# One of four steps issues its first fill ahead of the next block's scores

## The chip, the cores and the metric

The kernel runs on one core of a Trainium2 chip. The metric is the device time of one execution in microseconds (us); the time before is 1831.91 us, the median of 3 runs (1830.47 to 1837.54). Engines are called PE (TensorE), DVE (VectorE), ACT (ScalarE), POOL (GpSimd) and SP (SyncE, which here only issues transfers).

## The reference

```
x = x + 0.5 * ffn(layernorm(x))      # router: softmax, top 8 of 64, bias mix
x = x + attn(layernorm(x))           # gated linear attention with decay, below
x = x + 0.5 * ffn(layernorm(x))

# attn: 32 heads in 8 groups of 4, D = 128, L = 2048 tokens in chunks of 128
q, k, v = rope(x Wq), rope(x Wk), x Wv          # k, v shared by the 4 heads of a group
scores  = q k^T                                 # inside a chunk
y_intra = (scores * decay * dt) v
state   = state * exp(G_last) + (k * decay)^T (v dt)
y_inter = (q * exp(G)) state_of_the_chunk_before
y       = rmsnorm(y_intra + y_inter) * gnorm_w * silu(x Wg)
out     = y Wo
```

## The kernel before

The two ffn parts are a prologue (to about 125 us) and an epilogue (from about 1760 us). Between them stands the attention: for each of the 8 groups g there are 16 chunks n of 128 tokens, so 128 steps. Four chunks are a block b, and s = n mod 4 is the place of a chunk in its block. Every matrix product in bf16 is done as three (`mm3`, lines 298 to 300: high times high, low times high, high times low).

The projections of the next block (keys, four q heads, values, four gate parts) are ten **fills** of 12 matmuls or more each. They are spread over the four steps of the present block by the table `FILLS`: step s = 3 issues fill 8 in slot A and fill 9 in slot B (gate parts). Each fill goes to one of three PSUM banks; it waits until the fill two or three uses before has been read.

On PE a step is, in program order: the scores of chunk n+1 (`scores`), the fill of slot A, the read of the state (`read_state`), four transposes of the gated output of chunk n-1 (`turn_z`, L784), the weighting of the values and the new state (`attend`), the fill of slot B, and the output projection of chunk n-2 (`project_out`).

The names that the steps of the argument touch:
- `scores(g, n + 1)` writes bank `B_S`. At s = 3 chunk n+1 is the first of the next block, so it waits for all of that block's rounded q and k, last for QL of POOL (L1110), the low part of the last q head.
- DVE opens its step with `decayed(g, n + 1)` (L1307, four instructions that read `B_S`), then `add_out` (L1372), and at s = 3 then `keys_lo` (L1298, writes KDL, reads bank `B_T`).
- `B_T` is one bank, and transposed keys and transposed outputs share it. `turn_z(g, n - 1)` on PE waits on `turn_free` (L782); at s = 3 the count that it waits for is that of `keys_lo(b + 1)`.
- All engines run the groups in a hardware loop (`Fori(0, KVH - 1)`) whose body goes from n = 3 to n = 18, that is from step 3 of a group to step 2 of the next. The first instruction of its body is thus an s = 3 step. There are seven rounds: one entry, six turns, and after the exit the last group as straight code.

The order of instructions on each engine is written out by hand; only semaphores tie them together. Nothing is reordered at run time.

Of the kernel before, what the change touches and what calls it, by code (L numbers as in the profile page):

```python
# [29 lines left out]
BLK = 4  # L30
# [40 lines left out]
def filled(n, last):  # L71

    return {} if last and n // BLK == NB - 1 else FILLS[n % BLK]


def use_of(b, item):

    return NFILL * b + item
# [33 lines left out]
def build(nc, x, cos, sin, masks, wall, rwt, rb, eb2, wint, dtb, alog, gn, out):  # L112
    rows_dram = nc.dram_tensor("rows_dram", (NCH, KVH, GW), F32).ap()
    with ExitStack() as ctx:
# [177 lines left out]
        def wl_of(piece):  # L292

            return (wl_pool, POOL_LO.index(piece)) if piece in POOL_LO else (wl_dve, DVE_LO.index(piece))

        def mm3(out_, ah, al, bh, bl, first, last):

            nc.tensor.matmul(out_, ah, bh, start=first, stop=False)  # L298
            nc.tensor.matmul(out_, ah, bl, start=False, stop=False)  # L299
            return nc.tensor.matmul(out_, al, bh, start=False, stop=last)  # L300

        def bank(use):
            return RING[fill_bank(use)]
# [352 lines left out]
        def _(pe):  # L656
# [21 lines left out]
            def wkt(piece, k):  # L678
                return WH[:, piece, k * P:(k + 1) * P], WL[:, piece, k * P:(k + 1) * P]

            def bank_free(g, n, item, use):

                if n is None:
                    if use >= 3:
                        pe.wait_ge(ring_free.sem, ring_free.at(g, use - 3))
                elif n < PEEL:
                    pe.wait_ge(ring_free.sem, ring_free.at(g, use - AFTER_FILL_PEELED[item]))
                elif item in AFTER_FILL:
                    pe.wait_ge(ring_free.sem, ring_free.at(g, use - AFTER_FILL[item]))
                else:  # L690
                    pe.wait_ge(out_free.sem, out_free.at(g, n - 3))

            def fill(g, b, item, n, fresh, gw):

                use = use_of(b, item)
                out_bank = bank(use)
                bank_free(g, n, item, use)
                t0 = b % NB * TB
                if fresh:
                    piece = item if item <= PV_ else PG + KT - 1  # L700
                    pe.wait_ge(wh_ready.sem, wh_ready.at(gw, piece))
                    if item <= PV_:
                        signal, k = wl_of(piece)
                        pe.wait_ge(signal.sem, signal.at(gw, k))
                if item < PV_:
                    for k in range(KT):
                        wh, wl = wkt(item, k)
                        ins = mm3(out_bank[:, :], wh, wl, XTH[:, k, t0:t0 + TB], XTL[:, k, t0:t0 + TB], k == 0, k == KT - 1)
                elif item == PV_:
                    for s in range(BLK):  # L710
                        for k in range(KT):
                            t = t0 + s * P
                            wh, wl = wkt(item, k)
                            ins = mm3(out_bank[:, s * P:(s + 1) * P], XTH[:, k, t:t + P], XTL[:, k, t:t + P], wh, wl,
                                      k == 0, k == KT - 1)
                else:
                    t = t0 + (item - PG) * P
                    for k in range(KT):
                        if fresh and item == PG:
                            signal, i = wl_of(PG + k)  # L720
                            pe.wait_ge(signal.sem, signal.at(gw, i))
                        ins = mm3(out_bank[:, :], XTH[:, k, t:t + P], XTL[:, k, t:t + P], WH[:, PG + k, :], WL[:, PG + k, :],
                                  k == 0, k == KT - 1)
                ins.then_inc(ring_full.sem, 1)

            def turn_keys(g, b):
                if b:
                    pe.wait_ge(turn_free.sem, turn_free.at(g, k_turn(b) - 1))
                pe.wait_ge(qf_ready.sem, qf_ready.at(g, 5 * b))
                for s in range(BLK):  # L730
                    ins = nc.tensor.transpose(B_T[:, s * P:(s + 1) * P], KF[:, s * P:(s + 1) * P], IDF[:, :])
                ins.then_inc(kt_full.sem, 1)

            def scores(g, n):
                b, s = divmod(n, BLK)
                par, t = b % 2, s * P
                if s == 0:
                    pe.wait_ge(qh_ready.sem, qh_ready.at(g, 5 * b + 4))
                    pe.wait_ge(ql_ready.sem, ql_ready.at(g, 3 * b + 2))
                    pe.wait_ge(ql2_ready.sem, ql2_ready.at(g, 2 * b + 1))  # L740
                pe.wait_ge(p_ready.sem, p_ready.at(g, n - 1))
                mm3(B_S[:, :], KH[:, par, t:t + P], KL[:, par, t:t + P], QH[:, par, :, t:t + P], QL[:, par, :, t:t + P],
                        True, True).then_inc(scores_full.sem, 1)

            def read_state(g, n):
                b, s = divmod(n, BLK)
                par, t = b % 2, s * P
                if n % NCH:
                    pe.wait_ge(inter_read.sem, inter_read.at(g, in_event(n - 1)))
                    pe.wait_ge(sth_ready.sem, sth_ready.at(g, cs_event(n - 1)))  # L750
                    pe.wait_ge(stl_ready.sem, stl_ready.at(g, cs_event(n - 1)))
                    for h in range(G):
                        c = slice(h * P, (h + 1) * P)
                        ins = mm3(B_IN[:, c], QH[:, par, h, t:t + P], QL[:, par, h, t:t + P], STH[:, c], STL[:, c], True, True)
                    ins.then_inc(inter_full.sem, 1)

            def attend(g, n):
                b, s = divmod(n, BLK)
                par, t = b % 2, s * P
                pe.wait_ge(z_ready.sem, z_ready.at(g, n - 1))  # L760
                pe.wait_ge(ph_ready.sem, ph_ready.at(g, n))
                pe.wait_ge(pl_ready.sem, pl_ready.at(g, n))
                if s == 0:
                    pe.wait_ge(v_ready.sem, v_ready.at(g, b))
                    pe.wait_ge(ring_free.sem, ring_free.at(g, use_of(b, PV_)))
                for h in range(G):
                    c = slice(h * P, (h + 1) * P)
                    ins = mm3(B_PV[:, c], PH[:, n % 2, c], PL[:, n % 2, c], VH[:, par, t:t + P], VL[:, par, t:t + P], True, True)
                ins.then_inc(intra_full.sem, 1)
                if n % NCH == NCH - 1:  # L770
                    return
                pe.wait_ge(st_ready.sem, st_ready.at(g, cs_event(n - 1)))
                pe.wait_ge(wvh_ready.sem, wvh_ready.at(g, cs_event(n)))
                pe.wait_ge(wvl_ready.sem, wvl_ready.at(g, cs_event(n)))
                if s == 0:
                    pe.wait_ge(kdh_ready.sem, kdh_ready.at(g, b))
                    pe.wait_ge(turn_free.sem, turn_free.at(g, k_turn(b)))
                mm3(B_CS[:, :], KDH[:, par, t:t + P], KDL[:, par, t:t + P], WVH[:, :], WVL[:, :], True, True).then_inc(cs_full.sem, 1)

            def turn_z(g, n, last=False):  # L780
                pe.wait_ge(turn_free.sem, turn_free.at(g, z_turn(n, last) - 1))
                pe.wait_ge(z_ready.sem, z_ready.at(g, n))  # L782
                for h in range(G):
                    ins = nc.tensor.transpose(B_T[:, h * P:(h + 1) * P], YF[:, h * P:(h + 1) * P], IDF[:, :])  # L784
                ins.then_inc(zt_full.sem, 1)
# [34 lines left out]
            def step(g, n, last):  # L820
                b, s = divmod(n, BLK)

                def slot(x):
                    if x in filled(n, last):
                        fill(g, b + 1, filled(n, last)[x], n, b == NB - 1, g + 1)
                if not (last and n == NCH - 1):
                    scores(g, n + 1)
                slot("A")
                read_state(g, n)
                if n:  # L830
                    turn_z(g, n - 1, last)
                attend(g, n)
                if s == 1 and n >= 2:
                    project_out(g, n - 2, last)
                slot("B")
                slot("C")
                if s == 2 and filled(n, last):
                    turn_keys(g, b + 1)
                if s != 1 and n >= 2:
                    project_out(g, n - 2, last)  # L840
# [679 lines left out]
```

## Time and profile before

| what | value |
|---|---|
| median of 3 runs | 1831.91 us |
| profiled execution, device time | 1833.69 us |
| its span, first to last instruction | 1831.9 us |
| PE busy | 1687.1 us, 92% |
| DVE busy | 1436.0 us, 78% |
| POOL busy | 1221.6 us, 67% |
| ACT busy | 1137.8 us, 62% |

The profile is of one execution. Its page gives busy time for each engine, the waits and what ended them, and the granted TensorE clock as a share of full speed (1.00 is 2.4 GHz, 0.5 is 1.2 GHz). Ends of matmuls are modelled; their starts are read. So the times below go from start to start.

### The profile page before, as it was taken

The numbers are of one execution on the slowest core, as the hardware profiler recorded it, in microseconds if no ns is written. First come the engines' busy times: TensorE is split into PE (matmuls) and PEld (weight loads), VectorE is DVE, ScalarE is ACT, GpSimd is POOL, SyncE is SP. The second block draws the span as 40 slices with busy tenths as digits, with TensorE's granted clock in tenths as the row PEclk, the third lists the DMA queues.
The fourth block names the chain that finished last, engine by engine and source line by source line (L and its number), as shares of the span: only waits on it lengthen the run. The fifth ranks groups of instructions, "written<-read, shape, count | busy, mean of one in ns | idle before, by whom it ended". The sixth has DMA issues, their size and how long they took to land.

```text
span 1831.9 us, 39151 instructions
## 1 busy us (share of the span) xinstructions
PE 1687.1 (92%) x11451; PEld 970.9 (53%) x11652; DVE 1436.0 (78%) x3157; ACT 1137.8 (62%) x3012; POOL 1221.6 (67%) x1139
## 2 busy tenths in 40 slices
PE   5567999999999999999999999999999999999976
PEld 5533455555555455555555555555555555555544
DVE  6985778877887778777787778778888788777876
ACT  4545566666766667656676566656666566666653
POOL 1225677776777667767777667766877677766633
PEclk8888999999999999999999999999999999999997
DMA  4110101110120101110111102110111102100002
GB/s 172 35 34 19 47 19 59 47 43 24 30 69 25 44 24 53 47 49 19 42 60 34 37 18 64 42 43 24 42 58 34 34 19 70 36 31 23 24 1 92
DMA packets 38536, 77.29 MB, mean 42 GB/s; under 512 B 4768, under 2 KB 5792, under 8 KB 37152
## 3 DMA queue, kind: packets, MB, share of 16 engines
q1 hardware_dynamic: 38304, 74.47, 12.5%
q8 instruction: 113, 1.85, 0.4%
q14 instruction: 119, 0.97, 0.2%
HBM read 69.99 MB, written 4.46 MB: 41 GB/s over the span
## 4 chain that ended last, share of the span: by engine, by line
PE 52%; POOL 24%; issue 13%; DVE 5%; ACT 5%; POOLq 0%; DMA 0%; ACTq 0%; DVEq 0%
PE B L299 16%; PE B L300 15%; PE B L298 15%; POOL QS L1105 5%; POOL WL L1099 3%; POOL WVF L1128 3%; POOL ROWS L1118 3%; POOL WVL L1136 3%; POOL RR L1147 3%; PE B L784 2%; POOL QL L1110 2%; POOL RM L1144 1%; POOL KL L1112 1%; PE B L447 1%; ACT XN L417 1%
## 5 line engine op out<-in xcount | busy, mean ns | idle before, releaser
L1140 POOL TENSOR_TENSOR PL<-PF,PH 128x512 bf16<-128x512 f32 x128 | 155.8, 1217 | 345.0 <-ACT PH L937 345.0
L937 ACT ACTIVATE PH<-PF 128x512 bf16<-128x512 f32 x128 | 80.7, 630 | 359.4 <-DVE PF L1307 359.4
L300 PE MATMUL B<-WH,XTL 128*128 128x512 bf16 (+1 forms) x1024 | 286.3, 304 | 1.6
L299 PE MATMUL B<-WL,XTH 128*128 128x128 bf16 (+1 forms) x993 | 275.1, 302 | 2.2 <-issue 0.2
L298 PE MATMUL B<-WH,XTH 128*128 128x128 bf16 (+1 forms) x985 | 272.4, 302 | 3.2 <-POOL WL L1099 3.2
L299 PE MATMUL B<-XTL,WH 128*128 128x512 bf16 x639 | 242.8, 380 | 1.8
L298 PE MATMUL B<-XTH,WH 128*128 128x512 bf16 x607 | 230.6, 380 | 5.8 <-DVE QF L1273 3.5
L1105 POOL TENSOR_TENSOR QS<-QS,SIN 128x512 f32<-128x512 f32 x160 | 205.9, 1287 | 42.7 <-ACT QS L893 41.6
L300 PE MATMUL B<-XTH,WL 128*128 128x512 bf16 x609 | 231.6, 380 | 0.1
L1357 DVE SCALAR_TENSOR_TENSOR YF<-B,RR,G 128x128 f32<-128x128 f32 x512 | 144.1, 344 | 93.4 <-POOL RR L1147 93.4
L1307 DVE SCALAR_TENSOR_TENSOR PF<-B,DT,PF 128x128 f32<-128x128 f32 x512 | 143.4, 341 | 86.4 <-PE B L300 68.5
L298 PE MATMUL B<-WH,ZTH 128*128 128x512 bf16 x511 | 193.9, 379 | 0.1
L300 PE MATMUL B<-WH,ZTL 128*128 128x512 bf16 x511 | 193.7, 379 | 0.1
L299 PE MATMUL B<-WL,ZTH 128*128 128x512 bf16 x511 | 193.7, 379 | 0.1
L1316 DVE TENSOR_TENSOR YF<-B,EG 128x512 f32<-128x512 f32 x120 | 82.8, 690 | 113.9 <-PE B L784 112.2
L931 ACT ACTIVATE PF<-ROWS,NG 128x128 f32<-128x128 f32 x512 | 163.1, 391 | 12.4 <-POOL ROWS L1118 11.8
L1147 POOL TENSOR_TENSOR RR<-RM,HALF 128x4 f32<-128x4 f32 x128 | 155.4, 1214 | 19.0 <-POOL RM L1144 17.7
L1118 POOL TENSOR_TENSOR ROWS<-ROWS,AFTER 128x512 f32<-128x512 f32 x128 | 166.0, 1297 | 0.0
L960 ACT ACTIVATE YF<-B 128x128 f32<-128x128 f32 x512 | 133.9, 276 | 18.9 <-DVE B L1324 12.2
L298 PEld LDWEIGHTS B<-WH,XTH 128*128 128x128 bf16 x1024 | 101.3, 99 | 74.2 <-issue 7.9
L1136 POOL TENSOR_TENSOR WVL<-WVF,WVH 128x512 bf16<-128x512 f32 x120 | 138.7, 1156 | 0.7 <-ACT WVH L944 0.7
L1128 POOL TENSOR_TENSOR WVF<-VF,WJ 128x512 f32<-128x512 f32 x120 | 138.4, 1154 | 0.0
(158 smaller groups left out, 4475.8 us busy)
## 6 DMA issues: line engine op xcount, KB each, us to landing
ROWS<-rows_dram SPq DMA_DIRECT2D x128, 256.0 KB, 3.2
STAGE<-in_wall SPq DMA_DIRECT2D x112, 256.0 KB, 2.7
ACC<-in_x SPq DMA_DIRECT2D x4, 1024.0 KB, 7.0
out<-ACC SPq DMA_DIRECT2D x3, 1024.0 KB, 3.9
COS<-in_cos SPq DMA_DIRECT2D x1, 1024.0 KB, 12.0
SIN<-in_sin SPq DMA_DIRECT2D x1, 1024.0 KB, 13.8
out<-ACC SPq DMA_DIRECT2D x4, 256.0 KB, 2.5
EBF<-in_eb SPq DMA_DIRECT2D x1, 256.0 KB, 4.2
```

What stands on the lines that cost most here:

```text
L298: nc.tensor.matmul(out_, ah, bh, start=first, stop=False)
L299: nc.tensor.matmul(out_, ah, bl, start=False, stop=False)
L300: return nc.tensor.matmul(out_, al, bh, start=False, stop=last)
L931: ins = nc.scalar.activation(PF[:, c], ROWS[:, n % 2, c], ACT.Exp, bias=tab(NG, g, n)[:, h:h + 1], scale=-1.0)
L1105: nc.gpsimd.tensor_tensor(QS[:, sl, :], QS[:, sl, :], SIN[:, t0:t0 + TB], ALU.mult).then_inc(sin_ready.sem, 1)
L1118: nc.gpsimd.tensor_tensor(rows, rows, AFTER[:, None, :].broadcast_to([P, G, P]), ALU.add).then_inc(rows_masked.sem, 1)
L1128: nc.gpsimd.tensor_tensor(WVF[:, :, :], VF[:, b % 2, None, s * P:(s + 1) * P].broadcast_to([P, G, P]), tab(WJ, g, n)[:, :, None].broadcast ...
L1136: nc.gpsimd.tensor_tensor(WVL[:, :], WVF[:, :, :].rearrange("p h e -> p (h e)"), WVH[:, :], ALU.subtract).then_inc(wvl_ready.sem, 1)
L1140: nc.gpsimd.tensor_tensor(PL[:, n % 2, :], PF[:, :], PH[:, n % 2, :], ALU.subtract).then_inc(pl_ready.sem, 1)
L1147: nc.gpsimd.tensor_tensor(RR[:, :], RM[:, :], HALF[:, :], ALU.pow).then_inc(rr_ready.sem, 1)
L1307: ins = nc.vector.scalar_tensor_tensor(PF[:, c], B_S[:, c], dt[:, h:h + 1], PF[:, c], ALU.mult, ALU.mult)
L1357: ins = nc.vector.scalar_tensor_tensor(YF[:, c], B_PV[:, c], RR[:, h:h + 1], G2[:, s + b % 2 * (s == BLK - 1), c], ALU.mult, ALU.mult)
```

## The change

At s = 3 PE now issues the fill of slot A (fill 8) before the scores of chunk n+1. At s = 0, 1 and 2 the scores stay first. No other engine's code changes, and no semaphore count changes.

```
                 def slot(x):
                     if x in filled(n, last):
                         fill(g, b + 1, filled(n, last)[x], n, b == NB - 1, g + 1)
+                if s == BLK - 1:
+                    slot("A")
                 if not (last and n == NCH - 1):
                     scores(g, n + 1)
-                slot("A")
+                if s < BLK - 1:
+                    slot("A")
                 read_state(g, n)
                 if n:
                     turn_z(g, n - 1, last)
```

It touches 31 steps: n = 3, 7 and 11 of all eight groups and n = 15 of the first seven (the last block of the last group has no fills).

PE at an s = 3 step inside the loop body, before: the end of the output projection (ZTL), the scores (QH, QL with KH, KL), then the first of the 12 matmuls of fill 8 (WH, WL with XTH, XTL).

```order
L300 MATMUL B<-WH,ZTL 128x512
L738 REGISTER_ALU
L739 REGISTER_ALU
L740 REGISTER_ALU
L298 MATMUL B<-QH,KH 128x512
L299 MATMUL B<-QL,KH 128x512
L300 MATMUL B<-QH,KL 128x512
L689 REGISTER_ALU
L298 MATMUL B<-WH,XTH 128x512
L299 MATMUL B<-WL,XTH 128x512
L300 MATMUL B<-WH,XTL 128x512
```

The same place after the change, from the last three matmuls of fill 8 on, to the read of the state (STH, STL).

```order
L298 MATMUL B<-WH,XTH 128x512
L299 MATMUL B<-WL,XTH 128x512
L300 MATMUL B<-WH,XTL 128x512
L738 REGISTER_ALU
L739 REGISTER_ALU
L740 REGISTER_ALU
L298 MATMUL B<-QH,KH 128x512
L299 MATMUL B<-QL,KH 128x512
L300 MATMUL B<-QH,KL 128x512
L298 MATMUL B<-STH,QH 128x128
L299 MATMUL B<-STL,QH 128x128
L300 MATMUL B<-STH,QL 128x128
```

All 12 matmuls of the fill have moved ahead of the three of the scores; the read of the state now stands directly behind the scores.

PE at the head of the loop body (n = 3), before: the branch that closes the loop, then the waits of the scores and the scores.

```order
L299 MATMUL B<-WL,ZTH 128x512
L300 MATMUL B<-WH,ZTL 128x512
L844 UNCONDITIONAL_BRANCH
L844 ISA
L739 ISA
L740 ISA
L741 ISA
L298 MATMUL B<-QH,KH 128x512
L299 MATMUL B<-QL,KH 128x512
```

The same place after the change (the loop's line is now 847).

```order
L299 MATMUL B<-WL,ZTH 128x512
L300 MATMUL B<-WH,ZTL 128x512
L847 UNCONDITIONAL_BRANCH
L847 ISA
L298 MATMUL B<-WH,XTH 128x512
L299 MATMUL B<-WL,XTH 128x512
L300 MATMUL B<-WH,XTL 128x512
L298 MATMUL B<-WH,XTH 128x512
L299 MATMUL B<-WL,XTH 128x512
```

The fill is now the first work behind the branch, with no wait of the scores ahead of it.

DVE at an s = 3 step, which is the same before and after: behind L1307, which reads the scores, come the addition of an output and KDL.

```order
L1307 SCALAR_TENSOR_TENSOR PF<-B,DT,PF 128x128
L1307 ISA
L1307 SCALAR_TENSOR_TENSOR PF<-B,DT,PF 128x128
L1372 TENSOR_TENSOR ACC<-ACC,B 128x512
L1298 TENSOR_TENSOR KDL<-B,KDH 128x512
L1314 REGISTER_ALU
L1316 REGISTER_ALU
L1316 TENSOR_TENSOR YF<-B,EG 128x512
```

Nothing moved here: KDL still stands behind L1307 and L1372.

## Rows read from the trace of the kernel before

**Rows 1.** The page's head: span, and PE's busy time

```profile
span 1831.9 us, 39151 instructions
...
PE 1687.1 (92%) x11451; PEld 970.9 (53%) x11652; DVE 1436.0 (78%) x3157; ACT 1137.8 (62%) x3012; POOL 1221.6 (67%) x1139
```

**Rows 2.** Who waited for whom: us in total, times, longest us

```profile
PE B L298 <- POOL QL L1110: 32.0, 14, 3.5
...
PE B L784 <- DVE KDL L1298: 0.6, 1, 0.6
```

**Rows 3.** Timeline of PE, n = 15: start us, duration us, engine, line, operation

```profile
960.67 0.38 PE L298 MATMUL B<-WH,ZTH 128*128 128x512 bf16 x1
...
961.32 0.38 PE L298 MATMUL B<-QH,KH 128*128 128x512 bf16 x1
...
961.97 0.38 PE L298 MATMUL B<-WH,XTH 128*128 128x512 bf16 x1
...
964.56 0.22 PE L298 MATMUL B<-STH,QH 128*128 128x128 bf16 x1
...
965.23 0.60 PE L784 MATMUL B<-IDF,YF 128*128 128x128 f32 x4
```

**Rows 4.** Timeline of DVE in the same step

```profile
962.28 1.12 DVE L1307 SCALAR_TENSOR_TENSOR PF<-B,DT,PF 128x128 f32<-128x128 f32 x4 [0.80 <-PE B L300]
...
963.92 0.68 DVE L1298 TENSOR_TENSOR KDL<-B,KDH 128x512 bf16<-128x512 f32 x1
```

**Rows 5.** Timeline of all engines, the first turn of the loop (n = 3)

```profile
403.92 0.39 PE L298 MATMUL B<-QH,KH 128*128 128x512 bf16 x1 [3.11 <-POOL QL L1110]
...
407.76 0.68 DVE L1298 TENSOR_TENSOR KDL<-B,KDH 128x512 bf16<-128x512 f32 x1
...
408.58 0.65 PE L784 MATMUL B<-IDF,YF 128*128 128x128 f32 x4 [0.58 <-DVE KDL L1298]
```

**Rows 6.** Timeline of PE, n = 7

```profile
1062.93 0.38 PE L298 MATMUL B<-WH,ZTH 128*128 128x512 bf16 x1
...
1063.80 0.38 PE L298 MATMUL B<-QH,KH 128*128 128x512 bf16 x1
...
1067.71 0.61 PE L784 MATMUL B<-IDF,YF 128*128 128x128 f32 x4
```

**Rows 7.** Timeline of PE, n = 11

```profile
1112.46 0.38 PE L298 MATMUL B<-WH,ZTH 128*128 128x512 bf16 x1
...
1114.69 0.38 PE L298 MATMUL B<-QH,KH 128*128 128x512 bf16 x1 [1.42 <-POOL QL L1110]
...
1118.60 0.61 PE L784 MATMUL B<-IDF,YF 128*128 128x128 f32 x4
```

**Rows 8.** Timeline of PE and DVE, a typical turn of the loop (n = 3)

```profile
1012.57 0.39 PE L298 MATMUL B<-QH,KH 128*128 128x512 bf16 x1 [3.10 <-POOL QL L1110]
...
1014.82 1.13 DVE L1307 SCALAR_TENSOR_TENSOR PF<-B,DT,PF 128x128 f32<-128x128 f32 x4 [2.96 <-issue]
...
1016.45 0.68 DVE L1298 TENSOR_TENSOR KDL<-B,KDH 128x512 bf16<-128x512 f32 x1
...
1018.17 0.61 PE L784 MATMUL B<-IDF,YF 128*128 128x128 f32 x4
```

**Rows 9.** Line 844, PE's loop, around that turn: duration ns, start us

```profile
L844 PEldq COMPARE_BRANCH  x1: 3720/3720/3720, 1007.5 to 1007.5; - x1
...
L844 PEldq FUSED_REGOPS  x1: 50/50/50, 1011.3 to 1011.3; - x1
```

**Rows 10.** Timeline of PE, the longest turn of the six (n = 3)

```profile
1215.92 0.61 PE L298 MATMUL B<-QH,KH 128*128 128x512 bf16 x1 [3.10 <-POOL QL L1110]
...
1222.78 0.39 PE L784 MATMUL B<-IDF,YF 128*128 128x128 f32 x2
```

**Rows 11.** Timeline, n = 3 behind the exit of the loop

```profile
1623.38 0.38 PE L298 MATMUL B<-QH,KH 128*128 128x512 bf16 x1 [2.99 <-issue]
...
1625.87 0.69 DVE L1298 TENSOR_TENSOR KDL<-B,KDH 128x512 bf16<-128x512 f32 x1
...
1628.98 0.28 PE L784 MATMUL B<-IDF,YF 128*128 128x128 f32 x1
```

**Rows 12.** Busy us by stretch: PE, PEld, DVE, ACT, POOL; granted PE clock, DMA share, GB/s

```profile
1007.90:1017.90 10.00, 6.90 (x31) 2.79 (x29) 5.01 (x12) 2.65 (x8) 5.42 (x7) 0.83 0.30 85
...
1739.00:1749.00 10.00, 7.68 (x47) 4.57 (x47) 7.75 (x21) 5.78 (x23) 7.20 (x8) 0.83 0.01 2
1761.00:1771.00 10.00, 7.83 (x45) 4.58 (x45) 5.48 (x15) 6.21 (x17) 2.80 (x6) 1.00 0.01 2
```

More of the change, by code:

```diff
@@ L825, in slot @@
                         fill(g, b + 1, filled(n, last)[x], n, b == NB - 1, g + 1)
+                if s == BLK - 1:
+                    slot("A")
                 if not (last and n == NCH - 1):
                     scores(g, n + 1)
-                slot("A")
+                if s < BLK - 1:
+                    slot("A")
                 read_state(g, n)
```

## Prediction, made before the changed kernel ran

> **What bounds the kernel now.** I read the page's head first, then the list of waits, then the timeline of each kind of s = 3 step, and last the windows with the granted clock. PE is busy 1687.1 of 1831.9 us [rows 1], and most of the rest is prologue and epilogue; inside the attention part PE runs nearly without a break. So what delays PE there delays the end, and what frees PE there is gained. The largest wait of PE is that of L298 for POOL's QL: 32.0 us in 14 waits [rows 2]. It is the scores of the next block's first chunk, the very instruction that the change puts behind the fill. At n = 3 it waits 3.1 us and at n = 11 1.42 us (seven groups each: 7 x 4.52 = 31.6, the sum shown) [rows 5, 7, 8]; at n = 7 and n = 15 it hardly waits [rows 3, 6]. The second row in that list matters more than its size: L784, the transposes of `turn_z`, once waited 0.6 us for DVE's KDL. That is a wait which stands close behind PE in every s = 3 step.
>
> **The distances in a step.** Let E be the time at which PE could start what stands first in the step: the start of the last head's first product (960.67) plus three products of one third of 0.65 each, so 961.32 [rows 3]. From those rows: scores take 0.65 (961.32 to 961.97), fill 8 takes 2.59 (961.97 to 964.56), the read of the state 0.67 (to 965.23, where L784 starts). So before, L784 starts 3.91 behind the start of the scores. DVE starts L1307 0.96 behind the scores' start and ends KDL at 963.92 + 0.68 = 964.60, which is 3.28 behind it [rows 4]. In the one case where PE did wait for KDL, L784 started 408.58 against KDL's end at 407.76 + 0.68 = 408.44, so 0.14 later [rows 5]. L784 can therefore start no earlier than 3.28 + 0.14 = 3.42 behind the scores. Before, PE arrives at 3.91 and the slack is 0.49.
>
> **What the change does there.** The fill no longer lies between the scores and L784. PE arrives at L784 0.65 + 0.67 = 1.32 behind the scores, and must wait there until 3.42: a new wait of 2.10 us in every s = 3 step. Queued behind it on PE are `attend`, fill 9 and the output projection, and behind those the next step; nothing on PE can pass it. What stands on DVE between the scores and KDL is L1307 (four instructions) and L1372, so KDL moves with the scores and not with PE. With W for the time that the scores waited at E, L784 starts before at E + W + 3.91, and after at E + max(2.59, W) + 3.42. For W under 2.59 the step gets longer by 2.10 - W. Break-even is a wait of 2.10 us, and only n = 3 has one longer.
>
> - n = 15, W = 0: +2.10 [rows 3, 4]. Seven steps, and I price n = 11 of the last group the same, since that group stages no weights that make POOL late: 8 x 2.10 = 16.8.
> - n = 7, W = 1063.80 - (1062.93 + 0.65) = 0.22: +1.88 [rows 6]. Eight steps: 15.0.
> - n = 11, W = 1114.69 - 1113.11 = 1.58: +0.52 [rows 7]. Seven steps: 3.6.
> - n = 3 behind the exit of the loop [rows 11]: W is over 3, so the fill is hidden whole and the scores start where they did. L784 started 5.60 behind them (the clock fell in the fill). After, KDL ends at 1626.56, 3.18 behind the scores, and L784 starts at 3.32: -2.3. I take the entry alike, with 2.1 (its timeline reads so): together -4.4.
> - n = 3 at the six turns: here the wait for QL covers something else. PE's branch back starts at 1007.5 and lasts 3.72 us; the first register operation of the new round is at 1011.3 [rows 9]. The fill cannot start before that, and I add 0.2 for its own wait and weight load (my estimate, from the 0.2 us of one product). So fill at 1011.5, scores at 1014.1 instead of 1012.57 [rows 8]. DVE's L1307 started at 1014.82 with "issue" as the reason, 2.25 behind the scores instead of 0.96, since DVE had its own turn to make. After, it starts at 1014.1 + 0.96 = 1015.06. KDL ends 1017.13 - 1014.82 = 2.31 later, L784 starts at 1015.06 + 2.31 + 0.14 = 1017.5. That is 4.94 behind the old start of the scores. Before, it was 1018.17, 5.60 behind; the shortest turn has 408.58 - 403.92 = 4.66 [rows 5], the longest 1222.78 - 1215.92 = 6.86 [rows 10]. So +0.3 to -1.9 a turn, and I take -0.6, near the typical one: 6 x -0.6 = -3.6.
>
> The sum at full clock is 16.8 + 15.0 + 3.6 - 4.4 - 3.6 = **+27 us**.
>
> The Trainium skill (Advanced Engine Details and Errata, Control Flow Timing) gives about 108 ns for a compare-and-branch. By it the fill would be hidden at the turns too, the scores would stay where they are, L784 would be bound by DVE's own turn at 1017.27, and the sum would be some 1.5 us less. The row differs (3.72 us), and the row decides. The same skill (Runtime: NRT & Kernel Launch, Instruction fetch mechanics) says that a taken branch to a target outside the loaded pages has to fetch it first; that fits the row.
>
> **The clock.** In a turn PE's granted clock is 0.83 over 10 us, so (1 - 0.83) x 10 = 1.7 us are lost, a stretch at 1.2 GHz [rows 12]. That followed 3.1 us of idle PE. The loss is part of the 5.60 and 6.86 above, and I have counted it as gone. But the new 2.1 us waits could each bring such a fall. The nearest rows disagree: with PE busy 7.68 of 10 us the clock fell (0.83), with 7.83 it did not (1.00) [rows 12]. A step with the new wait is busy about 7.9. Below is none, above all 31: 0 to 53 us. I take four, nearer to the row that did not fall: +7 us.
>
> **What else moves.** No other engine issues in another order, and no DMA is moved or passed. The fill needs its bank free: gate part 6 was read by DVE one step before. The fill's reader (ACT's tanh) stands behind L937 on ACT, so it starts no earlier in the step. Behind L784 all distances stay as they were. PH and PL of chunk n+1 come up to 2.6 us later, but they are needed only in the next step's `attend`, some 10 us later by the timelines; so that costs nothing, and would cost what it exceeded 10 by.
>
> Sum: 27 + 7 = 34 us. The profiled execution took 1833.69 us with a span of 1831.9, so 1868 us for its like; the median of the runs is 1.8 us under the profiled one, which gives **1866 us**.
>
> **The rivals.**
> - **The change does what it seems to do** (faster): the fill covers the wait for QL and L784 does not bind. Then L784 starts 1.32 behind the scores: n = 15 unchanged, n = 7 -0.2, n = 11 -1.6, n = 3 about -4.3 at entry and exit and -2.7 at a turn. That is -2 - 11 - 9 - 16 = -38 us, 1794 us. For it speaks the 32 us row [rows 2]. Against it speak the count that `turn_z` waits for and the row in which L784 already waited for KDL [rows 5]. It decides where KDL would end under 1.4 us behind the scores; L1307 and KDL alone take 1.8. The Trainium skill (Perfetto Trace Analysis, Optimization Strategies) asks to keep the matmul engine busy, which is this rival's reason. Chance 0.04.
> - **The new wait is given back** (no change, about 1836 us): what waits on PE gives DVE, ACT and POOL time, and a later wait of PE shrinks. Against it: besides QL there is hardly a wait left on PE in this part to shrink [rows 2], and at n = 3 POOL's chain to QL hangs on the step just before. Chance 0.05.
> - **The clock falls behind nearly every new wait**: 27 + 53 = +80 us, 1912 us. For it: 7.68 busy with a fall; against: 7.83 without. Chance 0.11 for well over half of them, above 1890.
> - **The forecast**, +15 to +55 us: 0.80.
>
> **How the numbers follow.** The forecast without any fall is 1859, with some fifteen falls 1885. The low end takes 1852, for turns and clock both better than taken (about -7 us); the high end 1890 is half of the steps with a fall. Outside lie the rivals on the faster side (0.09) and most of the clock's (0.11). Within 0.5% (9 us, about what a measurement of this kernel can tell from none) lies only the second rival and a little of the forecast. So faster 0.04, same 0.06, slower 0.90.
>
> **What the changed profile would show.** The wait of L298 for QL gone or under 5 us. In its place L784 waiting for KDL, some 31 times, about 2.0 us each, some 60 us in total. At n = 15 L784 starts 3.4 behind the scores and 6.0 behind E instead of 3.9. At the turns the fill starts about 2.2 us behind E and not at once. The clock in a window around an s = 3 step is 1.00 in most. I am wrong if L784 starts directly behind the read of the state (then KDL's count is not what it waits for), or if the clock is 0.83 in most steps.

## The result, and the profile after

| | before | changed |
|---|---|---|
| median | 1832.87 us (4 runs, 1830.47 to 1837.54) | 1881.45 us (4 runs, 1877.38 to 1883.78) |
| profiled execution, its span | 1833.69, 1831.9 us | 1877.38, 1875.6 us |

The ratio is 1.0255, 95% interval 1.0235 to 1.0276: the kernel became 2.6% slower. The forecast was 1866 us in a range of 1852 to 1890.

The head of the changed kernel's page, against [rows 1]:

```profile
span 1875.6 us, 39352 instructions
...
PE 1705.8 (91%) x11652; PEld 972.3 (52%) x11652; DVE 1436.7 (77%) x3157; ACT 1136.1 (61%) x3012; POOL 1221.3 (65%) x1139
```

PE has more records here (11652 against 11451), since fewer are missing from this trace; its busy time is not to be compared to a few us. The waits are what changed. These are PE's in the changed kernel, against [rows 2] (lines behind the edit are three higher: KDL is L1301 and QL L1113; columns: us in total, times, longest us):

```profile
PE B L784 <- DVE KDL L1301: 60.5, 31, 2.3
...
PE B L298 <- issue: 11.8, 7, 2.1
...
PE B L298 <- POOL QL L1113: 0.9, 1, 0.9
```

The 32.0 us of waiting for QL have become 0.9. In their place stand 60.5 us of waiting for KDL, once in each of the 31 changed steps, and 11.8 us whose reason is "issue", nearly all of them at the six turns of the loop; before, this row had 3.9 us. The timeline of PE at an n = 15 step, to be laid beside [rows 3]:

```profile
1189.12 0.38 PE L298 MATMUL B<-WH,ZTH 128*128 128x512 bf16 x1
1189.77 0.38 PE L298 MATMUL B<-WH,XTH 128*128 128x512 bf16 x1
...
1192.36 0.38 PE L298 MATMUL B<-QH,KH 128*128 128x512 bf16 x1
...
1195.78 0.65 PE L784 MATMUL B<-IDF,YF 128*128 128x128 f32 x4 [1.93 <-DVE KDL L1301]
```

And DVE in the same step, beside [rows 4]:

```profile
1193.32 1.13 DVE L1310 SCALAR_TENSOR_TENSOR PF<-B,DT,PF 128x128 f32<-128x128 f32 x4 [3.40 <-PE B L300]
...
1194.96 0.68 DVE L1301 TENSOR_TENSOR KDL<-B,KDH 128x512 bf16<-128x512 f32 x1
```

The fill starts at 1189.77 and the scores 2.59 us later. L1310 starts 0.96 behind the scores and KDL ends at 1195.64, 3.28 behind them, both exactly as before. L784 starts 3.42 behind the scores and 6.01 behind the start of the step, where it was 3.91: +2.10. The same timeline at a turn of the loop, against [rows 8, 9]:

```profile
1030.53 0.38 PE L298 MATMUL B<-WH,ZTH 128*128 128x512 bf16 x1
1032.96 0.39 PE L298 MATMUL B<-WH,XTH 128*128 128x512 bf16 x1 [1.62 <-issue]
...
1035.56 0.38 PE L298 MATMUL B<-QH,KH 128*128 128x512 bf16 x1
...
1038.27 0.68 DVE L1301 TENSOR_TENSOR KDL<-B,KDH 128x512 bf16<-128x512 f32 x1
1039.08 0.65 PE L784 MATMUL B<-IDF,YF 128*128 128x128 f32 x4 [2.04 <-DVE KDL L1301]
```

The start of the last head in the turn of before that [rows 8] show:

```profile
1008.66 0.38 PE L298 MATMUL B<-WH,ZTH 128*128 128x512 bf16 x1
```

The loop's own line around the changed kernel's turn (duration ns, start us):

```profile
L847 PEldq COMPARE_BRANCH  x1: 3460/3460/3460, 1029.3 to 1029.3; - x1
L847 PEldq FUSED_REGOPS  x1: 50/50/50, 1032.9 to 1032.9; - x1
```

The fill cannot start before the branch is done, so PE has two gaps here, 1.62 and 2.04 us, where it had one of 3.1. From the start of the step (1030.53 + 0.65 = 1031.18) to L784 it is 7.90 us; before, it was 1018.17 - (1008.66 + 0.65) = 8.86, with a fall of the clock inside.

Last the granted clock. A "fall" is here a stretch at 1.2 GHz (0.5) after which the clock goes back to 1.00; one fall makes a window of 10 us read 0.83 and costs up to 1.7 us. Windows of the changed kernel (busy us of PE, PEld, DVE, ACT, POOL, then the clock), the first at an n = 11 step and the second at n = 15:

```profile
1136.00:1148.00 12.00, 10.06 (x67) 5.46 (x66) 8.57 (x20) 5.96 (x19) 8.16 (x8) 1.00 0.22 68
...
1188.00:1200.00 12.00, 10.07 (x60) 5.22 (x59) 6.58 (x15) 4.55 (x15) 4.90 (x6) 0.88 0.07 23
```

With the same wait (1.94 and 1.93 us) and the same busy time the clock fell in one and not in the other. Over all of the trace it fell behind 6 of the 23 waits for KDL at n = 7, 11 and 15: four times at n = 15, once at n = 7 and once at n = 11.

### The profile page after: what moved, and what is told of

It reads as the page before. It is cut to its first block, busy times and chain, and to the rows that moved or that the text cites. A ratio compares the mean times of both kernels' runs of the same rounds, so it can differ in the third digit from the quotient of the medians.

```text
span 1875.6 us, 39352 instructions
## 1 busy us (share of the span) xinstructions
PE 1705.8 (91%) x11652; PEld 972.3 (52%) x11652; DVE 1436.7 (77%) x3157; ACT 1136.1 (61%) x3012; POOL 1221.3 (65%) x1139
## 4 chain that ended last, share of the span: by engine, by line
PE 71%; POOL 11%; issue 8%; DVE 7%; ACT 2%; DVEq 0%; DMA 0%; POOLq 0%; ACTq 0%
PE B L298 21%; PE B L300 21%; PE B L299 21%; PE B L784 3%; POOL QS L1108 2%; POOL WL L1102 2%; POOL RR L1150 2%; POOL WVL L1139 1%; POOL WVF L1131 1%; DVE ACC L1375 1%; POOL ROWS L1121 1%; PE B L447 1%; DVE KDL L1301 1%; PE B L731 1%; DVE PF L1310 1%
## 5 line engine op out<-in xcount | busy, mean ns | idle before, releaser
L298 PE MATMUL B<-WH,XTH 128*128 128x512 bf16 (+1 forms) x1024 | 288.1, 305 | 14.7 <-issue 11.4
L299 PE MATMUL B<-WL,XTH 128*128 128x512 bf16 (+1 forms) x1024 | 287.7, 305 | 0.0
L1310 DVE SCALAR_TENSOR_TENSOR PF<-B,DT,PF 128x128 f32<-128x128 f32 x512 | 143.5, 341 | 148.3 <-PE B L300 143.0
L298 PE MATMUL B<-XTH,WH 128*128 128x512 bf16 x640 | 244.0, 381 | 3.5 <-DVE QF L1276 2.8
L300 PE MATMUL B<-XTH,WL 128*128 128x512 bf16 x640 | 243.8, 381 | 0.0
L934 ACT ACTIVATE PF<-ROWS,NG 128x128 f32<-128x128 f32 x512 | 163.1, 391 | 12.4 <-POOL ROWS L1121 11.9
```

What stands on the lines that cost most here:

```text
L934: ins = nc.scalar.activation(PF[:, c], ROWS[:, n % 2, c], ACT.Exp, bias=tab(NG, g, n)[:, h:h + 1], scale=-1.0)
L1310: ins = nc.vector.scalar_tensor_tensor(PF[:, c], B_S[:, c], dt[:, h:h + 1], PF[:, c], ALU.mult, ALU.mult)
```

## The experiments

The theory is that the 2.1 us waits of L784 for KDL are the loss, and that KDL is late only because it stands behind the reader of the scores on DVE. The first rival is that the late reader itself (PH and PL behind it) or the matmul order costs. The second rival is the clock's falls.

Where a time of one kind of step is given below, it is read in the profiled executions, from the scores of the step before to the scores of the step after, and compared with the same step before. In the three runs that leave whole kinds of steps alone (e2, e6 and e7) the untouched ones agree with before to 0.1 us, except at n = 3.

| run | what | median us | before in the same session | ratio, 95% interval |
|---|---|---|---|---|
| e1 | changed, KDL first on DVE | 1813.05 | 1830.92 | 0.9916 (0.9898 to 0.9934) |
| e2 | before, KDL first on DVE | 1835.30 | 1830.92 | 1.0020 (1.0005 to 1.0035) |
| e3 | changed, one operation less ahead of KDL | 1846.93 | 1830.92 | 1.0087 (1.0066 to 1.0108) |
| e4 | half of the fill ahead | 1839.99 | 1830.92 | 1.0051 (1.0035 to 1.0068) |
| e5 | before, KDL 1.2 us later | 1852.79 | 1833.36 | 1.0092 (1.0075 to 1.0109) |
| e6 | change at n = 3 only | 1837.24 | 1833.36 | 1.0019 (1.0002 to 1.0037) |
| e7 | change at n = 15 only | 1855.80 | 1833.36 | 1.0111 (1.0090 to 1.0131) |
| e8 | KDL first, fill ahead at n = 3 and 11 | 1808.62 | 1833.36 | 0.9859 (0.9842 to 0.9876) |
| e9 | KDL first, fill ahead at n = 11 only | 1831.76 | 1831.83 | 0.9990 (0.9969 to 1.0012) |

### KDL ahead of the reader of the scores

```
             def step(g, n, last):          # DVE
...
+                if s == 3 and now:
+                    keys_lo(g, b + 1)
                 if nxt:
                     decayed(g, n + 1)
...
-                if s == 3 and now:
-                    keys_lo(g, b + 1)
```

Expected: 

> The changed kernel, with KDL (keys_lo) moved to the head of DVE's step at s = 3, ahead of L1307; PE issues the fill first, as in the changed kernel. Theory (the 2.1 us waits of L784 for KDL are the whole loss, and KDL is late only because it stands behind L1307, which reads the scores): L784 waits for KDL no more, starts 1.32 us behind the scores, the wait for QL stays hidden, and the time falls below the kernel before: about 1795 us (38 under before). Rival 1 (what costs is that L1307 itself, and so PH and PL, come later): no gain from moving KDL, 1875 to 1885 us. Rival 2 (the clock's falls are the loss, set off by any unevenness): between 1840 and 1875 us.

Measured: 1813.05 us, 18 us under the kernel before (the two profiled executions are 24.5 us apart). PE at an n = 15 step of this run:

```profile
1149.08 0.38 PE L298 MATMUL B<-WH,XTH 128*128 128x512 bf16 x1
...
1151.67 0.38 PE L298 MATMUL B<-QH,KH 128*128 128x512 bf16 x1
...
1152.98 0.61 PE L784 MATMUL B<-IDF,YF 128*128 128x128 f32 x4
```

DVE in the same step:

```profile
1149.15 0.68 DVE L1301 TENSOR_TENSOR KDL<-B,KDH 128x512 bf16<-128x512 f32 x1
1152.63 1.12 DVE L1310 SCALAR_TENSOR_TENSOR PF<-B,DT,PF 128x128 f32<-128x128 f32 x4 [2.79 <-PE B L300]
```

L784 starts 1.31 behind the scores, with no wait, and 3.90 behind the start of the step. L1310 is as late as in the changed kernel (2.59 us later than before), and the kernel is faster all the same. So a late reader of the scores is not what costs, and neither is the order on PE; the first rival is out. The gain is half of the 38 us expected. At n = 7, n = 11, the entry and the exit the expected 2, 11 and 9 us did come (1.6, 11.1 and 8.2). The six turns gave 8.3 us instead of 16, and the seven n = 15 steps, for which nothing was expected, lost 7.0. Both are in this run's waits of PE (us, times, longest):

```profile
PE B L298 <- issue: 11.3, 7, 1.9
PE B L299 <- DVE ACC L1375: 7.3, 14, 0.7
...
PE B L784 <- issue: 4.8, 3, 1.8
...
PE B L784 <- DVE KDL L1301: 3.1, 3, 1.4
```

The turns still pay for the branch (11.3 us in this row, 3.9 before), and at all six of them L784 now waits until DVE has made its own turn (4.8 + 3.1 us in two rows). And PE, now earlier, meets 14 new waits of at most 0.7 us for an addition of DVE, seven at n = 14 and seven at n = 15. The last is the wait behind the wait: nobody waited there before.

Part of the gain is clock. Before, it fell behind the wait of the scores at n = 3 in seven of the eight groups, once for twice as long; in this run it falls in none of these steps. The one turn of before without a fall took 26.4 us and the others 26.9 to 28.6, so the falls made up some 5 us of the six turns. The turns of this run took 25.3 to 26.4.

The same edit in the order of before:

Expected: 

> The kernel before, with KDL moved to the head of DVE's step at s = 3 and nothing else. Theory: before the change L784 had 0.49 us of slack behind KDL, so moving KDL earlier there buys nothing: 1828 to 1834 us, and KDL ahead of L1307 costs nothing either. Rival (DVE's order costs by itself, either way): more than 5 us off the time before. This run tells whether a gain in the other run is that of KDL's place alone.

Measured: 1835.30 us, ratio 1.0020. That is 1 us above the expected range and 4 above the runs before in the same session, under the 5 us of the rival; the interval just leaves out 1. In the profiled execution all steps at n = 7, 11 and 15 take the time of before to 0.1 us, and only those at n = 3 scatter, as they do without an edit. So KDL's place alone buys nothing, as its slack of 0.49 us says; only together with the fill ahead does it pay.

### One operation less between the scores and KDL

```
-                if s != 2 and n >= PEEL:
+                if s < 2 and n >= PEEL:
                     add_out(g, n - 3, last)
...
                 if s == 3 and now:
                     keys_lo(g, b + 1)
+                if s == 3:
+                    add_out(g, n - 3, last)
```

Expected: 

> The changed kernel, with L1375 (add_out, 0.59 us from start to start) moved behind KDL at s = 3, so that only L1310 stands between the scores and KDL. Theory: KDL ends 0.59 us earlier behind the scores (2.69 instead of 3.28), each of the 31 waits of L784 falls from 2.0 to 1.4 us, the sum from 60.5 to about 42 us, and the time by 18 us plus a few falls of the clock that go too: 1855 to 1863 us. Rival 1 (late L1307 is what costs): unchanged, 1875 to 1885 us. Rival 2 (clock alone): as many falls, 1875 to 1885 us, or all of them gone, 1865 us with the waits unchanged.

Measured: 1846.93 us. PE's wait:

```profile
PE B L784 <- DVE KDL L1301: 42.5, 31, 2.0
```

The waits fell from 60.5 to 42.5 us, and that was forecast (42). The ratio to before fell from 1.0255 to 1.0087, which is 31 us, and only 18 of them are these waits. The rest fits the clock: the mean granted clock of the profiled execution is 0.972 against 0.966, which is (0.034 x 1875.6) - (0.028 x 1847.2) = 12 us less time lost. From n = 3 of the first group to the last changed step the changed kernel has ten falls (eight behind a wait for KDL, two inside a fill at a turn) and this run one, at a turn; nine times 1.7 is 15 us. So with waits 0.6 us shorter the clock fell less often too. The time is 8 us below the range that I expected, since the expectation had only a few falls go. The falls went together with the shorter waits; this run can't price them apart.

### Half of the fill ahead

```
+                half = s == BLK - 1 and filled(n, last)
+                if half:
+                    fill(g, b + 1, filled(n, last)["A"], n, b == NB - 1, g + 1, range(2))
                 if not (last and n == NCH - 1):
                     scores(g, n + 1)
-                slot("A")
+                if half:
+                    fill(g, b + 1, filled(n, last)["A"], n, b == NB - 1, g + 1, range(2, KT))
+                else:
+                    slot("A")
```

The fill's wait for its bank goes with the first half and its signal with the second.

Expected: 

> The kernel before, with half of fill 8 (6 of its 12 matmuls, 1.30 us) ahead of the scores at s = 3 and half behind them. By the formula of the theory L784 starts at E + max(1.30, W) + 3.42 or when PE arrives, E + max(1.30, W) + 2.61, whichever is later, against E + W + 3.91 before: n = 15 +0.8, n = 7 +0.6, n = 11 -0.5, n = 3 at entry and exit -2.2, at the turns about -0.6. Sum 8 x 0.8 + 8 x 0.6 - 7 x 0.5 - 4.4 - 3.6 = 0, so 1828 to 1840 us, with waits of L784 for KDL of 0.7 us each (about 20 us in total). Rival 1 (late L1307 costs in proportion to the work ahead of the scores): half of the loss of the full change, about 1857 us. Rival 2 (a loss of its own from breaking the order, whatever its size): 1875 us.

Measured: 1839.99 us, at the upper edge of the theory's range, and far from 1857 and 1875. PE's wait:

```profile
PE B L786 <- DVE KDL L1306: 26.7, 30, 2.4
```

26.7 us against the 20 expected. The loss is not in proportion to the work ahead (0.5% for half of the fill, 2.6% for the whole). The formula says why: 0.49 us of slack are used up first, and at n = 11 the first half still lies inside the wait for QL. By kind of step the profiled execution gives +0.85 at n = 15, +0.63 at n = 7 and -0.4 at n = 11, where +0.8, +0.6 and -0.5 were expected; what was too hopeful is again n = 3, with -2.6 us in all for -8.0.

### The disputed wait by itself

Two reductions on DVE ahead of KDL in the kernel before, nothing moved on PE:

```
                 if s == 3 and now:
+                    for i in range(2):
+                        nc.vector.tensor_reduce(SCR[:, i:i + 1], EG[:, :], AX.X, ALU.add)
                     keys_lo(g, b + 1)
```

Expected: 

> The kernel before, its order of TensorE unchanged, with two added reductions on DVE (128x512 to 128x1, into a scratch tile that nobody reads, my estimate 0.6 us each) between L1372 and KDL at s = 3. L1307 stays where it was; only KDL comes 1.2 us later. Theory: KDL ends 4.48 us behind the scores instead of 3.28, L784 can start at 4.62 instead of 3.91: +0.71 in the 23 or so steps outside n = 3, +0.3 to +1.2 at the six turns, nothing at entry and exit: 16 + 4 = +20 us, about 1851 us, and L784 waits for KDL some 25 times, about 0.6 us each. Rival 1 (late L1307, PH and PL cost, or the matmul order itself): no change, 1828 to 1836 us. This prices the disputed wait by itself, with nothing moved on PE.

Measured: 1852.79 us, 19 us over before. The timeline of DVE at an n = 15 step:

```profile
973.43 1.13 DVE L1308 SCALAR_TENSOR_TENSOR PF<-B,DT,PF 128x128 f32<-128x128 f32 x4 [0.81 <-PE B L301]
...
975.07 1.27 DVE L1424 TENSOR_REDUCE SCR<-EG 128x1 f32<-128x512 f32 x2
976.25 0.69 DVE L1299 TENSOR_TENSOR KDL<-B,KDH 128x512 bf16<-128x512 f32 x1
```

PE in it:

```profile
972.47 0.38 PE L299 MATMUL B<-QH,KH 128*128 128x512 bf16 x1
...
977.07 0.65 PE L785 MATMUL B<-IDF,YF 128*128 128x128 f32 x4 [0.53 <-DVE KDL L1299]
```

And its wait in total:

```profile
PE B L785 <- DVE KDL L1299: 17.2, 28, 1.7
```

L1308 starts 0.96 behind the scores, as before. KDL ends 4.47 behind them, and the transposes start at 4.60; 4.62 was expected. So a late KDL costs PE what the formula says, with PE's order and the reader of the scores as before. What stands behind KDL on DVE comes later too, but no other row of PE's waits inside the attention part grew by more than 1.7 us, and the steps at n = 7 and 15 are 0.72 and 0.73 us longer, which is the later L784 alone. This run and the first together show the cause from both sides.

### One kind of step alone

The condition `s == BLK - 1` of the change is replaced by `n % NCH == 3`, and in the next run by `n % NCH == NCH - 1`.

Expected for n = 3: 

> The changed kernel's edit at n = 3 alone, the one kind of step whose wait for QL (3.1 us) is longer than the break-even of 2.1 us; all others as before. Theory: entry -2.0, exit -2.3, six turns 0 together as the changed kernel's trace has them: -4 us, 1824 to 1832 us. Rival (the fill ahead costs everywhere alike): 8 of the 31 steps, a quarter of 46 us, +12: 1843 us.

Measured: 1837.24 us, 9 us above the middle of what the theory gave and 6 below the rival. The range was missed. PE's waits:

```profile
PE B L784 <- DVE KDL L1301: 17.1, 8, 3.0
PE B L298 <- issue: 12.1, 8, 1.9
PE B L298 <- POOL QL L1113: 11.0, 8, 1.5
```

The 22 us of waiting for QL at n = 3 have become 17.1 for KDL and some 8 more for the branch (12.1 in this row, 3.9 before). Entry and exit took 0.4 and 2.3 us less than before and the six turns 5.4 more in all, while no other step changed. And the clock still falls: of six windows of 20 us, one a turn, five show 0.91 and one 1.00; the first and the exception:

```profile
400.00:420.00 20.00, 16.43 (x97) 8.82 (x99) 11.82 (x30) 6.83 (x21) 8.92 (x9) 0.91 0.20 56
...
1220.00:1240.00 20.00, 17.85 (x121) 10.04 (x122) 13.02 (x33) 9.88 (x30) 11.02 (x11) 1.00 0.16 49
```

The -4 us that I had read off the distances to L784 counted falls before L784 as gone; they now come behind it, at 1.8 us each (0.09 x 20). A turn of this run took 28.3 to 29.0 us with such a fall and 26.4 without.

Expected for n = 15: 

> The changed kernel's edit at n = 15 alone (7 steps), where the scores had no wait for QL before. Theory: L784 2.1 us later in each, 7 x 2.14 = +15 us, plus some falls of the clock behind the new 1.93 us waits (four of the seven such steps had one in the changed kernel's trace, 1.7 us each: +7): 1845 to 1855 us. Rival (a quarter of the whole loss, as 7 of 31 steps): +11. Rival 2 (the loss comes from where QL was waited for): no change, 1831 us.

Measured: 1855.80 us, 22 us over before. In the profiled execution the seven steps are 2.2 us longer each, 15 us, and two of them 1.6 more by a fall behind the wait. Another 4.9 us stand at n = 3, which this edit doesn't touch: there the clock fell for twice as long at three turns and the exit, and before at one turn. Such long falls are in the kernel before as well, so the 15 and 3 us are the edit's, and whether the 4.9 are stays open. The rivals' 11 and 0 are out. The edge of the theory's range (1855) is passed by 1 us. PE's waits:

```profile
PE B L298 <- POOL QL L1113: 32.3, 14, 3.5
...
PE B L784 <- DVE KDL L1301: 13.5, 7, 1.9
```

### A version faster than both

```
-                if s == BLK - 1:
+                if n % NCH in (3, 11):
                     slot("A")
...
-                if s < BLK - 1:
+                if not (n % NCH in (3, 11)):
                     slot("A")
```

This is the first experiment's kernel, with the fill ahead only where the scores had to wait.

Expected: 

> KDL at the head of DVE's step (as in the first experiment) with the fill ahead of the scores only at n = 3 and n = 11, where the scores waited for QL. Theory: n = 7 and n = 15 gain nothing from the fill ahead (L784 stood 4.07 us behind the start of the last product before, and 4.07 with KDL first), apart from 0.2 us each at n = 7, so this gives the same time as the first experiment within 3 us: 1811 to 1817 us. Rival (the fill ahead is worth something in each step): over 1820 us.

Measured: 1808.62 us, ratio 0.9859: 1.4% faster than the kernel before, and 2 us under the expected range. It has 7 of the 14 small waits for DVE's addition, which are the new waits of the first experiment; the seven at n = 15 are gone, as the fill is not ahead there:

```profile
PE B L298 <- issue: 12.4, 8, 2.1
...
PE B L299 <- DVE ACC L1375: 4.6, 7, 0.7
```

And the clock no longer falls at n = 3; of six windows, one a turn, all show 1.00, as this one, and there is no fall from the entry on until n = 13 of the last group:

```profile
380.00:400.00 20.00, 17.44 (x130) 10.11 (x130) 15.27 (x32) 9.50 (x26) 12.67 (x11) 1.00 0.26 83
```

The same with the condition `n % NCH == 11`:

Expected: 

> As the version before it (KDL at the head of DVE's step, fill ahead of the scores), but with the fill ahead at n = 11 alone, 7 steps with a wait of 1.58 us and one without. Theory: those waits vanish and nothing else changes: -7 x 1.57 = -11 us, 1818 to 1824 us; the other 13 us or so of the version with n = 3 then lie at n = 3, where the long gap of PE and the fall of its clock go. Rival (most of the gain is at n = 11, or comes from KDL's place): within 4 us of 1809 us.

Measured: 1831.76 us (1821.34 to 1838.01 in ten runs), no different from before. That missed both expectations. PE's waits show that the waits at n = 11 did go, and what came:

```profile
PE B L298 <- POOL QL L1113: 22.2, 7, 3.5
...
PE B L299 <- DVE ACC L1375: 4.8, 7, 0.7
```

10 us of waits for QL are gone, 4.8 came back as waits for the addition: the wait behind the wait takes back near half of the gain. The rest went to the clock, at the turns that this edit doesn't touch. Its windows around two turns:

```profile
600.00:620.00 20.00, 19.08 (x113) 10.10 (x116) 10.79 (x28) 8.40 (x22) 8.78 (x10) 0.83 0.15 48
800.00:820.00 20.00, 16.85 (x90) 8.15 (x90) 12.61 (x31) 8.36 (x24) 9.92 (x11) 0.91 0.20 57
```

Of six windows three show 0.83, two 0.91 and one 1.00; 0.83 over 20 us are 3.4 us, two falls' worth. Why the slow stretch is twice as long behind some turns here stays open. In this trace the three long ones began 2.3 us after PE's gap began, and the short ones 2.8 to 3.3 us. The ten runs are 17 us apart, and the fastest, 1821.34, has a mean clock of 0.974 where the profiled one has 0.961. Between this run and the faster version lie 23 us. PE's waits in the two lists differ by about 8 of them (22.2 and 3.0 for QL and the exit here, 12.4 and 4.7 for the turns there). By kind of step the two profiled executions agree within 0.3 us in all at n = 7, 11 and 15, and the eight n = 3 steps differ by 20 us; there the clock fell in seven of the eight here, three times for twice as long, and in none in the faster version. So some 12 us are the clock's, as what is left of the 20 us; no run sets it by itself.

## Why the prediction was right, and which terms were off

- **The mechanism** was right: L784 waits for KDL in each of the 31 steps, 60.5 us (some 60 forecast), at 3.42 behind the scores. The first and fifth experiment show that nothing else is needed.
- **n = 15, 7 and 11.** At n = 15 the timeline gives 6.01 us from the start of the step to L784, the forecast's +2.10 to the hundredth. The three terms summed to 35.4 us; the trace gives 36.3 for these 23 steps when their six falls are taken off.
- **The entry, the exit and the turns.** This is the term that missed most. Entry and exit gave -1.8 and -2.3 us, where "-4.4" was put, but the six turns gave +3.4 for "6 x -0.6 = -3.6". The step that failed is "I have counted it as gone": the fall of the clock in a turn didn't go with the wait of 3.1 us. Before, five of the six turns had one, and [rows 12] show one of them. The window of the remaining turn, of the same length and with the same wait for QL, reads 1.00:

```profile
399.30:409.30 10.00, 6.32 (x44) 3.35 (x42) 4.96 (x12) 2.88 (x8) 5.46 (x7) 1.00 0.27 85
```

  In the changed kernel four of six had one: two inside the fill and two behind L784, where the distances of the prediction end. The two windows of the fills, and one with most of a fall behind L784 (1039.08) between them:

```profile
399.50:409.50 10.00, 7.90 (x34) 3.21 (x32) 3.56 (x7) 2.99 (x9) 5.46 (x5) 0.83 0.33 85
1030.00:1042.00 12.00, 8.34 (x54) 4.47 (x52) 6.67 (x15) 3.63 (x9) 7.44 (x8) 0.92 0.24 72
1448.00:1458.00 10.00, 7.97 (x35) 3.28 (x33) 3.54 (x7) 2.99 (x9) 5.46 (x5) 0.83 0.33 85
```

  The two turns without a fall took 26.6 and 26.8 us, 0.5 less than a typical one of before (26.9 to 27.3 us), which is the forecast's -0.6; the four with a fall took 28.1 to 28.6. In the turn shown PE won 1.0 us up to L784, and the step was 0.8 longer all the same. Four falls of 1.7 us are 6.8 of the 7.0 that the term missed.
- **The clock behind the new waits** was priced about right, on thin ground: "I take four", +7 us, against six falls, 10.2 us, at n = 7, 11 and 15. That four was near is luck, since no row of before says how often the clock falls behind a single wait of 2 us. Together the two terms make the forecast of 34 us some 44, with 43.7 measured between the profiled executions (1875.6 - 1831.9). The medians are 48.6 apart (1881.45 - 1832.87): the profiled execution of the changed kernel is the fastest of its four, and for the others there are no steps to read. All of this is counted against a forecast that took the old falls as gone. Counted as falls alone, the attention part had nine before and ten after (the long one taken as two), so the loss is in the waits and not in a greater number of falls, as the theory has it.
- **Break-even** at a wait of 2.10 us: n = 15 alone lost 22 us. n = 3 alone, with a wait of 3.1, was forecast to win and did not: the branch takes about 2 us of what the fill could hide at a turn, and the falls stayed. So the formula holds up to L784, but the whole price of a step has the clock in it.
- **The rival that the change would do what it seems to do** needed KDL out of the way. When KDL was moved it came half true: 1813 us, not the 1794 of the rival, since that had left out the waits at the turns and the next wait.

## What to carry to other kernels

Moving independent work ahead of a wait hides the wait, but it also delays everything that hangs on the waiting instruction. Follow its result to the readers, past the reader to what is queued behind it on that engine, and back to PE: here the second wait stood 0.49 us behind and cost 2.1 us a step where there had been no first wait to hide. Such a pair of edits can only be judged together: each alone lost or gave nothing, both together gave 0.8%, and 1.4% with the fill ahead only where the scores had waited. And a fall of the clock that stood behind the old wait is not gone with it: look whether the new gap has one too.

## What the runs showed of the hardware

A short gap of PE can cost more than its length: taking 0.6 us off each of 31 waits of about 2.0 us gave 31 us where 18 were in the waits, with a mean granted clock of 0.972 instead of 0.966. Whether the clock falls behind a given gap varies: it fell behind 6 of 23 single waits of 1.75 to 1.94 us, and two windows with PE busy 10.06 and 10.07 us of 12 had 1.00 and 0.88. In or behind the waits of 3.1 us at the turns of before it fell in five of six. A loop's branch took PE's sequencer 3.46 and 3.72 us in the two turns shown, of which about 2 us are not covered by the matmuls already queued (gaps of 1.62 to 2.10 us); the same branch at the loop's exit, where it is not taken, took 0.08 us. Ahead of a wait of 3.1 us it was free, and ahead of a fill it is paid for.
